# A deeper gather ring, eight banks and batched signals in two passes of a graph network kernel

## The reference

```python
# layers 0 and 2 (one along the edges, one against them)
agg = segment_sum(h[src], dst)            # layer 0
agg = segment_sum(h[edge_col], edge_row)  # layer 2: edge_row=src, edge_col=dst
z   = (1 + eps) * h + agg                 # then two dense products with batch norms and relu
# layer 1
a_in  = segment_sum(feat_in[src]  * iw[:, None], dst)
a_out = segment_sum(feat_out[dst] * ow[:, None], src)
# then gates and a tanh; layer 3: an MLP on every edge, summed by target node
```

## Time and profile before

| what | value |
| --- | --- |
| timed, median of 3 | 3428.03 us |
| profiled execution, span (its own time) | 4205.1 us |
| PE busy in the span | 2930.9 us (70%) |
| POOL busy | 2373.5 us (56%) |
| DVE busy | 2117.9 us (50%) |
| ACT busy | 1141.1 us (27%) |
| pass one, first to last gather begun | 649.9 to 1221.4 us |
| pass four, first to last gather begun | 2714.9 to 3290.4 us |

### The profile page before, as it was taken

How to read it: one execution, slowest core, us unless ns; L and a number is a source line. 1 busy time by engine, 2 the same in 40 slices (tenths; PEclk the granted TensorE clock), 3 DMA queues, 4 the chain that set the end, 5 groups by cost and what they waited for, 6 DMA issues and landing times. The chain is left out here.

```text
span 4205.1 us, 55362 instructions
## 1 busy us (share of the span) xinstructions
PE 2930.9 (70%) x11580; PEld 1849.8 (44%) x11581; DVE 2117.9 (50%) x6459; ACT 1141.1 (27%) x3023; POOL 2373.5 (56%) x2458
## 2 busy tenths in 40 slices
PE   3677776555542846677588887755554899988989
PEld 1233333333321434444333332433333548888878
DVE  6566664333320455444456655533333576667664
ACT  1466661000000330000000000300000356666662
POOL 3544445666667046666666666666666226666662
PEclk6788887667665867888799999976676999999999
DMA  3000002333320043333366666433333136666664
GB/s 123 2 1 1 1 1 74 90 89 90 90 56 2 20 139 88 101 106 105 109 176 180 177 176 178 138 89 89 87 91 86 34 124 186 187 188 185 189 187 143
DMA packets 184321, 438.94 MB, mean 104 GB/s; under 512 B 53924, under 2 KB 78623, under 8 KB 184233
## 3 DMA queue, kind: packets, MB, share of 16 engines
q0 software_dynamic: 135568, 372.32, 31.3%
q1 hardware_dynamic: 48665, 65.55, 4.7%
HBM read 403.39 MB, written 34.24 MB: 104 GB/s over the span
## 5 line engine op out<-in xcount | busy, mean ns | idle before, releaser
L834 POOL DMA_INDIRECT acc<-table,stg_idx x1170 | 1128.5, 965 | 767.8 <-issue 349.1
L2116 PE MATMUL psum<-acc,oh 128*128 x2600 | 871.4, 489 | 637.7 <-issue 456.5
L2116 PEld LDWEIGHTS psum<-acc,oh 128*128 128x128 f32 x2600 | 598.2, 244 | 912.3 <-issue 821.2
L1497 DVE TENSOR_TENSOR acc<-acc,psum 128x257 f32 (+1 forms) x660 | 276.0, 418 | 962.7 <-remote 565.4
L1032 ACT CAST stg_idx<-rec 128x2 int32 (+1 forms) x784 | 148.4, 193 | 2113.0 <-remote 841.2
L945 POOL DMA_INDIRECT TT<-qtable,stg_row x440 | 424.1, 964 | 282.4 <-PE psum L2428 150.9
L860 POOL DMA_INDIRECT H<-gtable,stg_idx x391 | 379.1, 970 | 199.5 <-issue 116.5
L2205 PE MATMUL psum<-H 125*128 125x440 bf16 x1600 | 375.5, 399 | 154.2 <-issue 48.2
L2137 PE MATMUL psum<-H,oh 128*128 x880 | 426.2, 630 | 79.8 <-issue 31.1
L810 POOL DMA_INDIRECT recs<-acc,sst_idx x290 | 284.6, 981 | 338.1 <-ACT acc L977 255.6
L2428 PE MATMUL psum<-oh,TT 128*128 128x128 f32 x3520 | 444.3, 277 | 34.7 <-issue 26.0
(11 more groups left out here) (277 smaller groups left out, 3210.7 us busy)
## 6 DMA issues: line engine op xcount, KB each, us to landing
acc<-table,stg_idx POOLq DMA_INDIRECT x1173
TT<-loc_dram SPq DMA_DIRECT2D x22, 320.0 KB
TT<-qtable,stg_row POOLq DMA_INDIRECT x440
Wm<-loc_dram SPq DMA_DIRECT2D x22, 320.0 KB
H<-gtable,stg_idx POOLq DMA_INDIRECT x391
gtable<-H SPq DMA_DIRECT2D x24, 256.0 KB
qtable<-H SPq DMA_DIRECT2D x24, 256.0 KB, 2.2
table<-H SPq DMA_DIRECT2D x8, 640.0 KB
```

Of the source, the lines that this page charges most:

```text
L834: pool.indirect_dma_start(out=dst[:, c, 0:D], out_offset=None, in_=src, in_offset=bass.IndirectOffsetOnAxis(ap=stg_idx[:, c:c + 1], axis=0 ...
L1497: V.tensor_tensor(at, at, sum_bank(j)[:, 0:w], ALU.add).then_inc(added, 1)
L2116: last = mm(sum_bank(j)[:, 0:w], oh[:, 2 * j + k, :], rows_flat[:, ds(start[j] + k * S, w)], start=(k == 0), stop=(k == 1))
```

## The change

For passes one and four only:

- The ring has `RING_D` = 14 places instead of 7. It lies in `acc` behind the sums of pass one (`deep_rows`), and has 14 landing semaphores `landed_d`. ACT stages 14 groups ahead of the transposes and then runs 13 turns of 14 groups, with two table loads of seven each. `stg_idx` has 28 columns.
- The units go through `BANKS` = 8 banks and eight one-hot pairs, the last three of which lie at the end of `H` (`more`). There are 27 blocks of eight and one of four, and the pairs are made `DLEAD` = 7 units ahead.
- PE raises `summed` by four with every fourth unit (`TOLD` = 4), and by nothing with the others.
- Each turn still loads two tables on PE and one on DVE, now for eight units. Pass four has no written-out turns.
- `sort` builds one more table for pass one (`deep_slot`, places modulo 14), with five short operations. The column of ones in the new ring is set just ahead of pass one, and PE waits for that once (`ones_ready`).

Passes two and three keep their rings, banks and updates. The diff, cut to its core:

```diff
+RING_D = 14
+DITS = GROUPS // RING_D
+BANKS = 8
+DEEP = PAIRS // BANKS
+DREST = PAIRS - DEEP * BANKS
+TOLD = 4
+DLEAD = BANKS - 1
...
+        deep_flat = acc[:, NB * S:NB * S + 2 * RING_D * S]
+        deep_rows = deep_flat.rearrange("p (c s) -> p c s", s=S)
...
-        stg_idx = sb("stg_idx", [P, 2 * RING_G], i32)
-        stg_row = sb("stg_row", [P, BODY], i32)
+        stg_idx = sb("stg_idx", [P, 2 * RING_D], i32)
+        stg_row = stg_idx[:, 0:BODY]
...
+        def hot_pair(j):
+
+            return [oh[:, 2 * j + h, :] for h in range(2)] if j < SP_IT else [more[:, 2 * (j - SP_IT) + h, :] for h in range(2)]
...
+            def relay_deep(turn):
+
+                short = [0] * (RING_D - 1) + [16]
+                with sp.Fori(turn * DITS, (turn + 1) * DITS - 1) as i:
+                    for j in range(RING_D):
+                        sp.wait_ge(landed_d[j], i * 32 + (32 - turn * short[j]))
+                        sp.sem_inc(arrived, 1)
...
-            gathers(3, table, rowsbuf)
+            gathers(3, table, deep_rows, RING_D, landed_d)
...
-            def stage_rest(n, first=1, end=GITS):
-
-                with act.Fori(first, end) as i:
-                    freed = loads(mybir.EngineType.Activation, free_tab[PASSES[n][0]], (i - 1) * RING_G, RING_G, PAIRS)
-                    for j in range(RING_G):
-                        act.wait_ge(summed, freed[j] + (n * PAIRS + SP_IT))
-                        stage_group(n, i * RING_G + j, j)
+            def stage_rest(n, ring):
+
+                with act.Fori(1, GROUPS // ring) as i:
+                    for j0 in range(0, ring, RING_G):
+                        freed = loads(mybir.EngineType.Activation, free_tab[PASSES[n][0]], (i - 1) * ring + j0, RING_G, PAIRS)
+                        for j in range(RING_G):
+                            act.wait_ge(summed, freed[j] + (n * PAIRS + SP_IT))
+                            stage_group(n, i * ring + (j0 + j), j0 + j)
...
+                    link(V.scalar_tensor_tensor(need_d, src[qd, 0:PAIRS], -1.0, cstart[qd, :], ALU.mult, ALU.add))
+                    link(V.tensor_scalar(deep_slot, need_d, -1.0, 4682.0, ALU.add, ALU.mult))
+                    link(V.tensor_scalar(deep_slot, deep_slot, 16, None, ALU.arith_shift_right))
+                    link(V.scalar_tensor_tensor(deep_slot, deep_slot, -float(RING_D), need_d, ALU.mult, ALU.add))
+                    V.tensor_scalar(deep_slot, deep_slot, -1.0, float(2 * S), ALU.add, ALU.mult)
...
+            def deep_pass(n):
...
+                def add_unit(b, j, block0):
+
+                    dve.wait_ge(summed, b * BANKS + (n * PAIRS + j + 1 + SP_IT))
+                    dve.wait_ge(added, b * BANKS + (n * PAIRS + j + SB))
+                    at = agg_flat[d][:, ds(block0, pass_width(n))]
+                    V.tensor_tensor(at, at, ps[j][:, 0:pass_width(n)], ALU.add).then_inc(added, 1)
+
+                def body(b, count, more):
+
+                    first = loads(mybir.EngineType.DVE, agg_tab[o], b * BANKS, count, (NB - 1) * S)
+                    for j in range(count):
+                        if j == 0 and count == BANKS:
+                            make_pair(b, DLEAD)
+                            copy_fields(b + 1, more)
+                        elif 0 < j <= more:
+                            make_pair(b + 1, j - 1)
+                        add_unit(b, j, first[j])
...
+            V.memset(deep_rows[:, :, D:D + 1], 1.0).then_inc(ones_ready, 1)
+            deep_pass(0)
...
+            def deep_units(n, b, count):
+
+                o = PASSES[n][0]
+                need = loads(mybir.EngineType.PE, need_tab[o], b * BANKS, count, GROUPS)
+                start = loads(mybir.EngineType.PE, deep_slot if n == 0 else slot_tab[o], b * BANKS, count, 2 * (RING_D - 1) * S)
+                w = pass_width(n)
+                for j in range(count):
+                    pe.wait_ge(hot, b * BANKS + (n * PAIRS + j + 1))
+                    pe.wait_ge(arrived, need[j] + n * GROUPS)
+                    if not isinstance(b, int) or b > 0:
+                        pe.wait_ge(added, b * BANKS + (n * PAIRS + j + 1 + SB - BANKS))
+                    for h, by in enumerate(hot_pair(j)):
+                        last = mm(ps[j][:, 0:w], by, deep_flat[:, ds(start[j] + h * S, w)], start=(h == 0), stop=(h == 1))
+                    if (j + 1) % TOLD == 0:
+                        last.then_inc(summed, TOLD)
...
-            sum_pass(3, 0, ITERS - 2)
-            ahead_tab = tables(3, ITERS - 2)
-            for k in (ITERS - 2, ITERS - 1):
-                tab = ahead_tab
-                for j in range(SP_IT):
-                    sum_rows(3, k, j, *tab)
-                    if j == 2 and k + 1 < ITERS:
-                        ahead_tab = tables(3, k + 1)
+            deep_pass(3)
```

More of the change, by code:

```diff
@@ L326, in gnn_kernel @@
         half = oh[:, CH_IT - 1, :]
+        more0 = 4 * NP + 260 - 2 * (BANKS - SP_IT) * P
+        more = Hm[:, more0:4 * NP + 260].rearrange("p (c n) -> p c n", n=P)
+        assert w0 + 2048 <= more0
         own_row = acc[:, spare:spare + HID]
@@ L631, in _ @@
             move_offsets(1)
[L633 to L638 removed]
+            def relay_deep(turn):
[3 more added lines that the diff above has]
+                        sp.wait_ge(landed_d[j], i * 32 + (32 - turn * short[j]))
                         sp.sem_inc(arrived, 1)
[L640 to L641 removed]
+                for j in range(RING_D):
+                    sp.wait_ge(landed_d[j], (turn + 1) * DITS * 32 - (turn + 1) * short[j])
                     sp.sem_inc(arrived, 1)
@@ L827, in scatter_half, with gather_pair @@
                     scatter(k, sst_idx[:, s:s + 1], sst_rec[:, s, :])
-            def gather_pair(i, j, src, dst):
-                pool.wait_ge(staged, i * RING_G + j + 1)
+            def gather_pair(i, j, src, dst, ring, done):
+                pool.wait_ge(staged, i * ring + j + 1)
                 pool.sem_inc(stages_begun, 1)
@@ L836, in gather_pair, with gathers @@
                         in_offset=bass.IndirectOffsetOnAxis(ap=stg_idx[:, c:c + 1], axis=0)
[L837 to L846, removed]
+                    ).then_inc(done[j], 16)
+            def gathers(n, src, dst, ring, done):
+                its = GROUPS // ring
+                with pool.Fori(n * its, (n + 1) * its - 1) as i:
+                    for j in range(ring):
+                        gather_pair(i, j, src, dst, ring, done)
+                for j in range(ring - 1):
+                    gather_pair((n + 1) * its - 1, j, src, dst, ring, done)
+                pool.wait_ge(staged, (n + 1) * GROUPS)
                 pool.sem_inc(stages_begun, 1)
-                c = 2 * RING_G - 2
+                c = 2 * ring - 2
                 pool.indirect_dma_start(
@@ L851, in gathers @@
                     in_offset=bass.IndirectOffsetOnAxis(ap=stg_idx[0:END_ROWS, c:c + 1], axis=0)
-                ).then_inc(landed[RING_G - 1], 16)
+                ).then_inc(done[ring - 1], 16)
             def gather_wide(g, j, half):
@@ L889, in _ @@
             table_ready(0)
-            gathers(0, table, rowsbuf)
+            gathers(0, table, deep_rows, RING_D, landed_d)
             pool.wait_ge(late_saved, 1)
@@ L900, in _ @@
             table_ready(1)
-            gathers(1, table, rowsbuf)
+            gathers(1, table, rowsbuf, RING_G, landed)
             pool.wait_ge(gates_kept, UNITS + 1)
@@ L2214, in _ @@
             drained("z0")
-            sum_pass(0)
+            pe.wait_ge(ones_ready, 1)
+            deep_pass(0)
             pass_end(0)
```

83 lines of the change are left out of this document (57 added, 26 removed).

## The result

| | before | changed |
| --- | --- | --- |
| timed, median of 9 | 3427.56 us | 3436.17 us |
| lowest to highest | 3425.06 to 3429.03 | 3433.95 to 3438.46 |
| ratio, 95% interval | | 1.0025 [1.0017, 1.0033] |
| profiled execution, span | 4205.1 us | 3432.4 us |

The account below looks back on a forecast made before the run. POOL's gathers were taken to set the pace in passes one and four, with some real stall. 3428.0 us less 31 of stall plus 4.6 of costs gave 3402 us; range 3330 to 3458, likeliest case 3385 to 3425.

Parts of the forecast that it names:

- The timed passes, bounded: Timed passes one and four: gather period 1.149 us, POOL's step 1.109, so 31 us of stall in the two.
- x: What the recording adds outside the four passes: between 0 and 510 us, with the middle, 255, used.
- PE's sum: PE in passes one and four: busy time plus table loads, 435 us against POOL's 434; fewer loads worth 26 us, no further term.
- The ring of 14: POOL's stall in passes one and four goes: -31 us taken, bounds 0 and -163.
- waits on the indices under 10 us: Sign in the trace after: POOL's waits on ACT's `stg_idx` under 10 us in passes one and four, from 88.6 and 86.0.
- Updates by four: At the end of passes one and four, DVE's last four adds start only after PE's last unit: +1.4 us each, +2.8.
- the price of the written-out turns: Pass four's last block: two table loads, 2.5 us, ahead of four units, hidden behind 7 gathers; if not, +2.5 us.
- Eight banks and pairs, ACT, table building: Banks, pairs and ACT's seven more copies: nothing, covered by POOL; table building +1.6 us, ones column before pass one +0.2.
- A: No stall in timed runs, POOL's step is a pass's whole period; only the costs are left, 3432.6 us; chance 0.29.
- C: PE becomes the bound in passes one and four, granted clock under 0.62: slower, 3455 us; chance 0.18.
- D: Gathers slow under DVE's bunched work, 0.99 us instead of 0.957, median over 0.98: 3457 us; chance 0.03.
- The estimate from the Trainium skill: PE's increments, 165 fewer at 26 ns: 4.3 us less a pass; 3393 us if PE paced throughout, held not likely.

Follow-up runs that it names:

- the control: The kernel before with one register operation more (max with 0) ahead of each wait against a table's value: 3427.20 us, ratio 0.9997.
- half-gather runs: Changed kernel without each group's second gather in passes one and four: 2948.17 us; the same with ring of 7 and updates by one: 2944.08 us.

## Why the prediction was wrong, by its own steps

**The failed step: "The timed passes, bounded".** The prediction asked rightly how much of the first trace was the recording's, and rightly held most of the stall to be so. Then it shared out the 777 us with two choices of the middle: x = 255 outside the passes, and half of the gap of 0.30 us. That made a step of 1.109 us and a period of 1.149, and so a stall of 31 us for the change to remove. Both choices fell. In recordings that cost nothing the step is 1.26 us, and passes one and four of the kernel before (with the maximum) are 491.8 and 493.8 us, with stalls of 0.4 and 1.2. The prediction had the first figure itself, "390 steps of 1.261 us are 491.8", and then left it. The four passes of the control sum to 491.8 + 496.4 + 493.9 + 493.8 = 1976 us from first to last gather. In the first trace these stretches were 571.5 + 587.2 + 577.4 + 575.5 = 2312 us, 336 more, and their stalls 343 us against 9 in the control. So x is 777 - 336 = 441, at 86% of its bound of 510. The trace had a sign of this: the gap was 0.30 us ahead of nearly every gather, 350 times in a sum of 125.9, while the stalls were rare and irregular. Here, what was the same hundreds of times belonged to the engine, and the excess came in lumps.

**The second leg, PE's sum.** 326 us of busy PE plus 109 of loads, "level" with POOL's 434, was taken as support. The half-gather runs refute it: all of PE's work is done in 250 us. A busy time at a granted clock of 0.71 is not work that needs that long; it fell by 121 us where the clock was 0.99. The loads that the change saves were off the path.

**The ring of 14.** Its value is nil, because there was nothing to remove. Its sign in the trace, waits on the indices under 10 us, came true by luck: the control with the ring of 7 has 7.0 and 7.3 us in a quiet recording. Whether 14 places would have bridged the pauses of the disturbed one isn't shown, since no recording of a deep ring was disturbed.

**Updates by four.** The mechanism and the place were right, the size was low: +1.4 a pass was taken, +1.9 and +2.2 us measured as PE's idle time, 4.1 for 2.8. The prediction read the state before from the earlier trace rows, where the four adds of the disturbed recording already ran in a row, 0.62 us apart; in the control three of them lie beside the products, and PE idles 0.61 us. Timed, 4.8 us come back with updates by one. The tails as a whole are 4.6 us longer; the rest of that is when the last products end, 3.77 us after the last gather's start in pass four before and 4.54 after. It is not the price of the written-out turns that went: with updates by one at the end only, and no written-out turns, the products end after 3.84 us. In pass four 0.4 us of idle time (0.99 against 0.61) stay even with updates by one, and their cause is open.

**Eight banks and pairs, ACT, table building.** Covered, as said: with a ring of 7 or 14 and updates by one the kernel is at 1.0003 [0.9994, 1.0012] and 1.0006 [0.9997, 1.0015]. The 1.6 us for the tables and the 0.2 for the ones column would fit into that, and aren't shown.

**The rivals.** A, no stall in timed runs, is what happened, by the sign that the prediction had set for it (a timed run over 3425 us with the profiled stall gone): 3432.6 us foretold, 3436.2 measured. Of the 3.6 us between them 1.3 are the tail term; the rest is open. A had a chance of 0.29. C and D did not occur: the granted clock of the passes was 0.74 and 0.73, as in the control (0.75 and 0.73), and the median gather 0.953 and 0.957 us. The estimate from the Trainium skill, 4.3 us a pass for 165 fewer increments (page "TensorE: Matmul & The Clock Gate", section "The cost: per-tile semaphore tail"), is not tested by these runs: TensorE isn't the pace, so a saving inside a pass would not show. All they show is that the kernel with more increments is 4.8 us faster, by its tails.

**What stays open.** Why one recorded execution was 777 us longer, while thirteen others were within 5 us of their timed medians, and whether it was the recording at all or something else that disturbed that one execution. Where the last 3 to 4 us of the changed kernel are, beyond the 4.1 of the tails; the first gather of pass one began 1.5 us later in its recording, but that start varies by as much between kernels that are the same up to there.

## What to carry to other kernels

When a profiled execution is much longer than the timed runs, record again first: here thirteen of fourteen recordings were quiet. If there is only the one, don't divide the excess evenly. In this case the gap that stood ahead of every instruction was the engine's own, and the rare waits on signals were the excess; work out the pass's period first with the stalls alone taken away. A deeper ring helps only where the engine that fills it was ever held up; cut the depth, or that engine's work, to see where the next bound is, before building more of it. Signals by the batch cost their batch at the end of every pass, so let the last batch signal one by one.

## What the runs showed of the hardware

The time of a register load of a table does not simply grow with the number of values: on TensorE five values took a median of 1.23 us and eight 0.77, while on ScalarE four took 0.31 (ring of 4) and seven 1.54. Through 16-bit views of every second word eight took 2.09 on TensorE, but five 1.22 and ScalarE's seven 1.51, much as through the plain view. Their lines for the changed kernel in pass one (ns min/median/max):

```profile
L575 PEldq TENSOR_LOAD <-acc x28: 513/765/779, 440.2 to 919.9; - x28
L575 DVEq TENSOR_LOAD <-acc x28: 350/598/867, 440.8 to 924.9; - x28
...
L575 ACTq TENSOR_LOAD <-acc x26: 957/1540/1560, 439.3 to 877.9; - x26
```

The first is to be compared with the earlier trace rows: a block of eight loads in less time than a turn of five, where the prediction had taken 1.233 us for both. Nothing in the passes hangs on it, as POOL is the pace.

An indirect DMA of 128 rows kept POOL busy for 0.95 to 0.96 us (median) and the next began 0.30 us later, so 1.26 us from start to start, in passes of 391 as in passes of 196 gathers, and mostly landed 2.7 to 2.8 us after its start.

A product with a one-hot in `oh` took a median of 572 ns in pass one of the changed kernel, at a mean granted clock of 0.74, and 379 ns in the same pass of the half-gather run with the ring of 14, at 0.99. The mean of 0.74 is made of stretches at 1.2 and at 2.4 GHz.
